# Moving the second layer's keys and values from behind the experts into the routing

## What is computed

```python
x = x + tanh(g_xattn[0]) * L0_xattn(layernorm(x), ctx)   # 16 heads of 64
x = x + tanh(g_ffn[0])   * L0_ffn(layernorm(x))          # 8 experts, top 2 of them
x = x + tanh(g_xattn[1]) * L1_xattn(layernorm(x), ctx)   # 8 heads of 128
x = x + tanh(g_ffn[1])   * L1_ffn(layernorm(x))          # coupling network, 3 cycles
```

## Time and profile before

| | us |
|---|---|
| median of 3 runs | 1012.97 (1012.3 to 1014.51) |
| the profiled execution, its own time | 1014.85 |
| its span | 1013.0 |
| PE busy | 933.9 (92%) |
| DVE busy | 569.5 (56%) |
| ACT busy | 468.2 (46%) |
| POOL busy | 371.5 (37%) |

### The profile page before, as it was taken

One profiled execution on the slowest core, in us unless ns is written; L12 is line 12 of the kernel. 1 busy time (PEld: TensorE's weight loads), 2 busy tenths in 40 slices (PEclk: granted clock), 3 DMA queues, 4 the chain that ended last, 5 costly groups with the idle time before them and its releaser, 6 DMA issues.

```text
span 1013.0 us, 20489 instructions
## 1 busy us (share of the span) xinstructions
PE 933.9 (92%) x6821; PEld 849.0 (84%) x6822; DVE 569.5 (56%) x1319; ACT 468.2 (46%) x1451; POOL 371.5 (37%) x498
## 2 busy tenths in 40 slices
PE   5999999999999755999999996899999999989995
PEld 3589999999998755999999974799999999975662
DVE  7554555545455464334444346777777776663273
ACT  0255555555555211444434433656555655544442
POOL 5153343433433103222222115655555643423132
PEclk9899999999999856999999998899999999999987
DMA  9400000000000044977667733100000000000002
GB/s 280 131 1 2 1 0 1 2 1 2 1 0 1 7 167 148 319 258 251 244 244 250 255 109 106 28 22 21 13 21 10 22 1 1 2 1 1 1 0 83
DMA packets 37503, 76.15 MB, mean 75 GB/s; under 512 B 5101, under 2 KB 23777, under 8 KB 37313
## 3 DMA queue, kind: packets, MB, share of 16 engines
q1 hardware_dynamic: 34033, 66.03, 19.6%
q0 software_dynamic: 3408, 9.31, 2.7%
HBM read 66.02 MB, written 9.31 MB: 74 GB/s over the span
## 4 chain that ended last, share of the span: by engine, by line
PE 85%; DVE 8%; POOL 2%; ACT 2%; issue 1%; DMA 1%; POOLq 0%; DVEq 0%; SPq 0%; ACTq 0%
PE banks L1527 14%; PE banks L487 11%; PE banks L489 11%; PE banks L488 11%; PE banks L521 8%; PE banks L495 6%; PE banks L506 6%; PE banks L513 3%; PE banks L636 3%; PE banks L1738 2%; PE banks L353 1%; PE banks L1342 1%; PE banks L1742 1%; PE banks L1517 1%; PE banks L1724 1%
## 5 line engine op out<-in xcount | busy, mean ns | idle before, releaser
L1527 PE MATMUL banks<-region_b,region_a 128*128 128x128 f32 x1248 | 147.8, 277 | 1.1 <-ACT region_b L1560 0.5
L1527 PEld LDWEIGHTS banks<-region_b,region_a 128*128 128x128 f32 x1248 | 144.6, 194 | 1.8 <-issue 0.9
L1102 ACT ACTIVATE region_a<-banks,negmax 128x154 f32<-128x154 f32 x256 | 96.0, 388 | 91.0 <-DVE negmax L851 89.8
L1257 POOL TENSOR_TENSOR region_a<-region_a,recip 128x512 f32<-128x512 f32 x64 | 66.5, 1039 | 178.7 <-DVE recip L857 178.7
L1292 POOL TENSOR_TENSOR region_a<-region_a,recip 128x640 f32<-128x640 f32 x64 | 80.2, 1253 | 107.7 <-DVE recip L971 107.5
L1606 DVE SCALAR_TENSOR_TENSOR region_a<-banks,region_b,region_a 128x128 f32<-128x128 f32 x156 | 43.9, 345 | 108.9 <-PE banks L1527 108.9
L521 PE MATMUL banks<-region_a 128*128 128x128 f32 x768 | 96.6, 275 | 1.9 <-DVE oT_low L874 1.8
L521 PEld LDWEIGHTS banks<-region_a 128*128 128x128 f32 x768 | 91.0, 192 | 2.9 <-issue 2.2
L495 PE MATMUL banks<-region_a 128*128 128x308 f32 x256 | 77.1, 425 | 0.0
L487 PE MATMUL banks<-Wo_high,oT_high 128*128 128x256 f32 x256 | 76.0, 297 | 0.9 <-DVE oT_low L874 0.9
L1161 ACT CAST pT_high<-banks 128x640 fp32r<-128x640 f32 x64 | 44.4, 694 | 66.8 <-PE banks L636 66.8
(11 more groups left out here) (249 smaller groups left out, 2470.0 us busy)
## 6 DMA issues: line engine op xcount, KB each, us to landing
region_a<-in_L_ffn_W SPq DMA_DIRECT2D x39, 1024.0 KB
y_slots<-region_b SPq DMA_DIRECT2D x39, 128.0 KB
W<-in_L_ffn_W SPq DMA_DIRECT2D x1, 4096.0 KB, 17.4
region_b<-in_L_xattn_Wq SPq DMA_DIRECT2D x2, 1024.0 KB
xn_rows<-region_b SPq DMA_DIRECT2D x1, 2048.0 KB, 8.5
out<-x SPq DMA_DIRECT2D x4, 512.0 KB, 2.9
region_b<-in_L_xattn_Wk SPq DMA_DIRECT2D x2, 768.0 KB, 7.3
region_b<-in_L_xattn_Wv SPq DMA_DIRECT2D x2, 768.0 KB
```

The lines of the kernel that those rows point to most:

```text
L1102: e = act.activation(pr[:, j, 0:L.keys], scores[:, g % 2, u, i * L.keys:(i + 1) * L.keys], ACT.Exp, bias=negmax[:, g % 2, j:j + 1], accum_ ...
L1257: pool.tensor_tensor(whole, pr[:, :, 0:split], rc.broadcast_to([P, L.hs, split]), ALU.mult)
L1527: mm = pe.matmul(banks[:, 2 * r + part, m * P:(m + 1) * P], W1[:, r, k, cols], xgT[:, r, k, :], start=(k == 0), stop=(k == DK - 1))
```

## The change

- SP loads the second layer's Wk and Wv after half of the first attention, into the half of K0 and V that is no longer read (`Wk1`, `Wv1`). DVE shifts the context there as well, in two of the steps of the tenth tile (t = 9).
- The 16 units are made in the routing: two v units ahead of its loop, a k unit behind four of its passes, four k units and two v units behind the ranking, the two r units behind the 32 token products. ACT copies each out of its bank, in f32, to `K1` and `V1`; nothing is split there.
- The splits are made from these copies: the query weights in four parts during slots 33 to 36 of the experts (ACT and POOL), K, V and Wo in six parts (`L1_PARTS`) by ACT and DVE behind the last slot. POOL's subtractions of Wq and Wo there are gone.
- Wq and Wout of the second layer are loaded ahead of the experts and not behind them. W1's buffers 1 and 2 and `b2` lie where Wk1 and Wv1 were, so SP loads them behind the last unit. `a_act` and `act_sum` have one buffer in place of three.
- `mixed_pair(2)` moves behind the first `row_max`. Two banks in place of four take the router's results.

```diff
+        KV1_UNITS = [("v", 0, 0), ("v", 0, 1)] + [("k", c, 0) for c in range(NC)] + [("v", 1, 0), ("v", 1, 1)] + \
+            [("r", 0, half) for half in range(2)]
+        KV1_AFTER_RANK, KV1_AFTER_TOKENS = 6, 12
+        def key_unit(n):
+
+            return (2 + n // 4 - 1,) if n % 4 == 1 and 5 <= n <= 17 else ()
...
         def pe_pairs(pe):
             t0, s0 = NT, STEPS
-            pe_kv1(pe, "vk")
             pe.wait_ge(sem("xn_ready"), t0 + 2)
             pe_pair_x(pe)
-            pe_kv1(pe, "r")
-            pe.wait_ge(sem("Wq_split"), 2)
+            pe.wait_ge(sem("query_low"), QUERY_PARTS)
             pe.wait_ge(sem("xt2_sb"), 1)
             pe_pair_q(pe, 0)
...
+            for n in range(4):
+                part_low(n)
             mixed_pair(0)
-            dve_kv1(dve, L1, "k", range(4, NC))
+            part_low(4)
...
+            part_low(5)
             pair_q_rest(1, 0)
             row_max(0, 0)
+            mixed_pair(2)
             pair_q_rest(2, 1)
...
-                    if first and n in (1, 2):
-
-                        pool.wait_ge(sem("Wo_high"), 2)
-                        part = slice((n - 1) * NC // 2, n * NC // 2)
-                        pool.tensor_tensor(Wo_low[:, part], Wo1[:, part], Wo_high[:, part].bitcast(F32),
-                                           ALU.subtract).then_inc(sem("Wo1_split"), 1)
...
             sp.wait_ge(sem("owner_ready"), 1)
-            for j in range(RING):
-                load_w1(j, j)
+            load_w1(0, 0)
+            sp.wait_ge(sem("kv1_ps"), len(KV1_UNITS))
+            load_w1(1, 1)
+            sp.dma_start(b2[:], t_in["L0_ffn_b2"].rearrange("e n -> (e n)").partition_broadcast(P)
+                         .rearrange("p (e n) -> p e n", e=E)).then_inc(sem("b2_in"), 16)
+            load_w1(2, 2)
             sp.wait_ge(sem("hg_ps"), 1)
...
+                    if query_part(j) is not None:
+                        n = query_part(j)
+                        pool.wait_ge(sem("query_high"), n + 1)
+                        pool.tensor_tensor(Wq_low_parts[:, n], Wq1_parts[:, n], Wq_high_parts[:, n].bitcast(F32),
+                                           ALU.subtract).then_inc(sem("query_low"), 1)
```

More of the change, by code:

```diff
@@ L403, in pe_kv1 @@
-        def pe_kv1(pe, kinds):
-            for n, (kind, a, half) in enumerate(KV1_UNITS):
-                if kind not in kinds:
-                    continue
+        KV1_UNITS = [("v", 0, 0), ("v", 0, 1)] + [("k", c, 0) for c in range(NC)] + [("v", 1, 0), ("v", 1, 1)] + \
+            [("r", 0, half) for half in range(2)]
+        KV1_BANKS = (6, 7) + (6, 7, 6, 7) + (0, 1, 2, 3) + (7, 0) + (4, 5)
+        KV1_FREE = (0, 0) + (1, 2, 3, 4) + (0, 0, 0, 0) + (6, 7) + (0, 0)
+        KV1_AFTER_RANK, KV1_AFTER_TOKENS = 6, 12
@@ L407, in pe_kv1 @@
+        def key_unit(n):
+            return (2 + n // 4 - 1,) if n % 4 == 1 and 5 <= n <= 17 else ()
+        def pe_kv1(pe, units):
+            for n in units:
+                kind, a, half = KV1_UNITS[n]
                 if n == 0:
-                    pe.wait_ge(sem("wv_in"), 32)
+                    pe.wait_ge(sem("kv_in1"), 32)
                 if kind == "k" and a == 0:
-                    pe.wait_ge(sem("wk_in"), 32)
                     pe.wait_ge(sem("ctx_shifted"), 1)
-                keys = slice(a % 2 * 2 * P, a % 2 * 2 * P + KEYS)
@@ L421, in pe_kv1, with act_kv1 @@
                         left = ctxT[:, k, a * P:(a + 1) * P] if kind == "v" else ctx_rem1[:, k, :]
-                        mm = pe.matmul(bank, left, Wv[:, k, half * 512:(half + 1) * 512], start=(k == 0), stop=(k == 1))
+                        mm = pe.matmul(bank, left, Wv1[:, k, half * 512:(half + 1) * 512], start=(k == 0), stop=(k == 1))
                 mm.then_inc(sem("kv1_ps"), 1)
-        def remainder_rows(j):
-            return slice(64 * j, 64 * j + 64)
-        def act_kv1(act, L, kinds, chunks=range(NC)):
-            for n, (kind, a, half) in enumerate(KV1_UNITS):
-                if kind not in kinds or a not in chunks:
-                    continue
+        def act_kv1(act, units):
+            for n in units:
+                kind, a, half = KV1_UNITS[n]
                 act.wait_ge(sem("kv1_ps"), n + 1)
-                bank = kv1_bank(n)
+                bank = banks[:, KV1_BANKS[n]]
                 if kind == "k":
-                    last = act.activation(K_high[:, a, :], bank[:, 0:KEYS], ACT.Copy, scale=L.scale)
+                    last = act.activation(K1[:, a, :], bank[:, 0:KEYS], ACT.Copy, scale=L1.scale)
                 elif kind == "v":
-                    last = act.copy(V_high[:, half * 4:half * 4 + 4, a, :], bank.rearrange("p (c n) -> p c n", c=4))
+                    last = act.copy(V1[:, half * 4:half * 4 + 4, a, :], bank.rearrange("p (c n) -> p c n", c=4))
                 else:
@@ L1174, in exponentials @@
                 e.then_inc(sem("p_exp"), 1)
[L1176 to L1180 removed]
+            act.wait_ge(sem("ey_ps"), SLOTS)
+            for raw, high, low, c in L1_PARTS:
+                act.copy(high[:, c:c + 4], raw[:, c:c + 4]).then_inc(sem("l1_high"), 1)
             x_high(1)
[L1182 removed]
             pair_q_high(1, 0)
@@ L1455, in act_routing @@
                 act.copy(xeT[:, t % 4], banks[:, t % 4, 0:D].rearrange("p (k n) -> p k n", k=DK)).then_inc(sem("xet_sb"), 1)
+                act_kv1(act, key_unit(t))
+            for n in range(NT, NT + 3):
+                act_kv1(act, key_unit(n))
+            act_kv1(act, range(KV1_AFTER_RANK, KV1_AFTER_TOKENS))
             act.wait_ge(sem("margin_ready"), 1)
@@ L1458, in act_routing, with query_part @@
             act.activation(table[:, 0:1], zero_eps[:, 0:1], ACT.Silu)
+            act_kv1(act, range(KV1_AFTER_TOKENS, len(KV1_UNITS)))
         ROUNDS = SLOTS // RING
+        QUERY_PARTS = 4
+        QUERY_FROM = RING * (ROUNDS - 2)
+        Wq1_parts, Wq_high_parts, Wq_low_parts = [
+            w.rearrange("p k n -> p (k n)").rearrange("p (t n) -> p t n", t=QUERY_PARTS)
+            for w in (Wq1, Wq_high[:], Wq_low[:])]
+        def query_part(j):
+            return j - QUERY_FROM if isinstance(j, int) and 0 <= j - QUERY_FROM < QUERY_PARTS else None
         def slot_bodies(eng, emit):
@@ L1602, in gated @@
                 e = owner_of(dve, j)
+                if not (isinstance(j, int) and j == 0):
+                    dve.wait_ge(sem("act_low"), j)
                 dve.wait_ge(sem("silu_done"), j + 1)
```

245 lines of the change are left out of this document (119 added, 126 removed).

## The result

The changed kernel takes 1004.71 us (median of 4 runs, 1002.99 to 1006.44). The kernel before took 1013.01 us beside it (4 runs, 1012.3 to 1014.51). The ratio is 0.9916, with a 95% interval of 0.9896 to 0.9937, so the change gives 8.3 us. Forecast were 999.0 us, a gain of 14.0. The profiled execution took 1002.99 us with a span of 1001.2.

The account below looks back on a forecast made before the run. PE was taken as full inside the stages, with time lost at two borders, before and behind the experts. Terms -11.5, -2.8 and +0.3 gave -14.0, so 1013.0 became 999.0 us; range 992 to 1010.

Parts of the forecast that it names:

- Rivals 1 and 2: Routing loop: half clock throughout, 1015.4 us, chance 0.12; or clock falls and k units lift it, 1006, chance 0.10.
- rival 3: Behind the experts, DVE's wide subtractions hold up POOL's gathers: +4.6 us, 1003.6 in all, chance 0.13.
- rival 4: Behind the experts, POOL and DVE bound the first steps, so the 3.6 us wait only moves: 1006 to 1009, chance 0.10.
- First border, forecast -2.8: Routing up to the third hidden layer of the experts: all terms there together save 2.8 us.
- loads of W1 and b2, +1.4: Behind the last unit, late loads delay DVE's first gate and PE's first W2 product: 1.4 us cost.
- r units, +1.8: Two r units behind the token products take 6.3 us in a 4.5 us wait for the first gather: 1.8 cost.
- Warm first slot, -2.1: The experts' first slot starts at a raised clock; its 32 records and the turning save 2.1 us.
- Second border, -11.5: Behind the experts: all terms there together save 11.5 us, bounds -8 and -15.
- +0.4 for the gathers: Behind the experts, POOL's four gathers beside DVE's subtractions take 0.1 us longer each: 0.4 us cost.
- The half clock at +1.0: Behind the experts, PE has idled, so products from the turning on run at half clock: 1.0 us cost.
- `mixed_pair(2)`, -2.5 and +3.0: Behind the experts, moving it shortens the `q_low` wait by 2.5 us but delays work behind `row_max` by 3.0.
- DVE in the first attention, +0.3: First attention: 2.2 us of added DVE work, ahead of a full PE, costs 0.3 us.

Follow-up runs that it names:

- v_behind: Changed kernel with the two v units moved from ahead of the routing's loop to behind the ranking; 1015.74 us.
- v_behind_warm: v_behind plus seven filler products, results unused, in the gap ahead of the routing's loop; 1003.23 us.
- b2_wait: Changed kernel with DVE's wait for `b2` moved from ahead of its first gate to where it first adds `b2`; 1003.91 us.
- mix_old: Changed kernel with `mixed_pair(2)` put back ahead of the first `q_low`; 1005.96 us.
- lows_late: Changed kernel with DVE's six subtractions moved away from POOL's gathers, to behind the turning; 1009.37 us, one execution.
- filler: Changed kernel with 28 filler products on PE between the last slot and the first pair's turning; 1006.13 us.
- after_again: The changed kernel run once more, unchanged; 1004.77 us.
- before_warm: The kernel before, without the change, plus seven filler products in the gap ahead of the routing's loop; 1007.34 us.
- r_early: Changed kernel with the two r units ahead of the 32 token products, so the loads start earlier; 1006.28 us.
- head4: Changed kernel with early r units, the moved `b2` wait, W1's third buffer loaded behind the k units and `b2` after the first gather; 1002.74 us.

## Why the prediction was too high on the gain

Rivals 1 and 2 did not come about: PEclk was 1.00 from the v units to the loop's end. That half of the argument was right, and the pair v_behind and v_behind_warm shows its reason. The price given for the other side (1015.4 forecast, 1015.74 measured for v_behind) hit that closely by luck: slot 2 came 11.0 us later than before (69.1 against 58.1) and not 13.6, and from there to the next pair's turning 10.3 us were won and not 11.5. By distances v_behind costs 1.2 us, forecast 2.4.

Of the others, rival 3 came about in part (2.8 us of its 4.6), and so did rival 4: of the 3.6 us wait for POOL 2.3 stay. The time is inside the range, but outside the 995 to 1002.5 of the forecast itself.

What failed is the size of terms. By distances, before to after:

- *First border, forecast -2.8.* Slot 2 stands at +0.8, the end of the experts' hidden layers at +1.2 (251.2 against 250.0). The miss of 3.6 to 4.0 us is the largest. Of it, 2.4 us are the term "loads of W1 and b2, +1.4": from the last unit to slot 2 passed 14.8 us and not 12.4. The chain gate, conversion, subtraction, W2 product was named rightly. But I had let `b2` arrive 8 us behind the last unit, and DVE's gate began 9.8 us behind it: 1.2 until SP issued the load and 8.6 until the gate. That is 1.8; the rest is the fall of the clock behind PE's wait, with which the way from the first W2 product to slot 2 took 2.39 us (1.59 in b2_wait). b2_wait removes both; mix_old has the wait without the fall. About 1.0 us more is the loop: 14.8 us (345.67 to 360.4) in place of 9.6 + 4.2 = 13.8. Between the two marks another 0.4 are lost, as slot 2's own 32 records took 4.42 us and not 3.74. The last 0.2 us I have not assigned; the r units' 6.50 us against 6.3 would be of that size.
- *r units, +1.8.* 6.50 us measured, 6.3 forecast, in a wait of 4.5.
- *Warm first slot, -2.1; six units behind the ranking, 0.* 3.84 us against 5.66 for the 32 records. PE's wait for the token products fell from 14.1 to 4.6 us: the cover was there.
- *Second border, -11.5.* Measured -9.6 from the end of the experts' hidden layers to the next pair's turning (24.3 + 36.9 before, 21.2 + 30.4 after). Right were the gathers (2.8 us from the last issue, 606.83, to the mix at 609.63, forecast 3.1), the mix (1.00 us for two), the query (2.61 us behind the turning, forecast 2.5), `q_low` (1.49, forecast 1.5) and the loss of the fall of the clock behind the Wo wait. Wrong were the step "+0.4 for the gathers" and the fifth subtraction, put at nothing beside POOL's rstd: lows_late shows 2.8 us for what the subtractions do to POOL, 1.9 at the gathers and 0.9 at rstd. The half clock at +1.0 is not contradicted by filler, which won 0.9 with a clock that was higher but not full.
- *`mixed_pair(2)`, -2.5 and +3.0.* mix_old shows that the two cancel within 0.2 us; I had them cancel within 0.5.
- *DVE in the first attention, +0.3.* Nothing of it is seen: at the same clock of 0.95 in the start-up the turning of `b1` came at 343.3 us in after_again and at 343.5 in before_warm.
- *Coupling network.* From its first product to the end, after has lost another 0.7 us to before in its profile (111.5 against 110.8). I had no term for it and did not test it.

The misses of 4.0, 1.9 and 0.7 us, less the 0.3, are the 6.3 by which the gain behind the turning of `b1` falls short of 14.0. They leave 7.7 us, by distances (667.0 to 659.3); the medians say 8.3, and the 0.6 between them is less than the start-up's scatter.

One number in the text on record is wrong without consequence: there are 14 units, not 16 (4 v, 8 k, 2 r; the diff and the records count them so).

Seen from before_warm, the account reads differently than I wrote it. The clock in the routing is worth 6.5 us by itself, with nothing moved. With the gap filled on both sides, moving 21 us of PE work out of one border and into the other gives 2.6 us by medians and only 0.9 by distances (660.2 to 659.3): 9.0 won from slot 2 to the next pair's turning (252.9 to 243.9), 58.9 - 51.6 = 7.3 paid at slot 2, of which b2_wait gives 4.0 back, and 0.8 lost behind. A gain of this size is not clear of the scatter.

## What to carry to other kernels

Before a large move of work is credited with a gain, the cheap part should be tried alone: here a gap of 2 to 3 us ahead of a stretch of small products went with half clock through the whole stretch, and seven filler products in it bring 6.5 of the 8.3 us. A wait written at the head of an engine's list holds everything behind it, so it belongs at the first instruction that reads what is waited for, above all when the load behind it has just been made later. Where work is moved into another engine's idle time, its neighbours on a shared path (here POOL's gathers beside DVE's wide subtractions, and a small gather beside bulk loads) are part of its price.

## What the runs showed of the hardware that was not expected

- Dense PE work at 0.50 does not lift the clock by itself in this stretch: 25.1 us without a gap in v_behind, 308 columns wide products among it. The same instructions behind 3.9 us of filling ran at 1.00. After the Trainium skill (TensorE: Matmul & The Clock Gate, What's actually happening), activity should have released it; the trace of v_behind disagrees, as that of before did. Elsewhere the clock did rise under dense work: the first slot's 32 records took 5.66 us in the kernel before and later ones 3.74. What in the loop keeps it low was not tested.
- The clock also fell without a gap: in before_warm from 1.00 to 0.50 within 355.5 to 357.2 us, with PE busy throughout, in the last turnings and products of eight columns.
- The start of the kernel is not the same twice. The window from 20 to 56 us, first in the changed kernel's first profile, then in after_again's, then in v_behind_warm's:

```profile
20.00:56.00 36.00, 30.49 (x146) 20.05 (x146) 24.98 (x86) 11.26 (x41) 12.70 (x12) 1.00 0.46 143
```

```profile
20.00:56.00 36.00, 30.19 (x133) 19.84 (x132) 24.80 (x85) 10.24 (x38) 11.99 (x11) 0.95 0.45 139
```

```profile
20.00:56.00 36.00, 30.19 (x97) 19.21 (x96) 21.36 (x81) 7.41 (x24) 9.48 (x8) 0.81 0.45 139
```

  At 1.00, 0.95 and 0.81 PE got through 146, 133 and 97 records in the same 36 us, and the turning of `b1` then came at 341.9, 343.3 and 347.8. The code ahead of it is the same in the three. A spread of 6 us is enough for most of the scatter between the runs of one kernel; that it is the cause there is not shown, as one execution of each was profiled. It is why a step of 2 us is better read from distances inside a profile.
- A gather of 128 rows that was issued with free queues let PE start after a wait of 4.5 us; issued beside loads at 425 GB/s, after one of 7.7 (r_early); with fewer loads beside it, again after 4.6 (head4).
